# A graph network stack on one core: the RMS row sums spread by a repeated column instead of a diagonal, and the layer norm's small steps moved from VectorE to GpSimd

## The reference, cut to what matters

```python
def _layernorm(x, axis=-1, eps=1e-5):
    m = jnp.mean(x, axis=axis, keepdims=True)
    v = jnp.var(x, axis=axis, keepdims=True)
    return (x - m) / jnp.sqrt(v + eps)

# layer 0: graph convolution with degree scaling, then batch norm over all graphs
# layer 1: 8-head attention with the adjacency as its mask
# layer 2:
neighbor_sum = jnp.einsum('bnm,bmd->bnd', adjacency, x)
agg = epsilon * x + neighbor_sum
h = jnp.einsum('bnd,dh->bnh', agg, W1) + b1          # 1024 hidden features
h = jax.nn.silu(_rmsnorm(h, rms_weight))             # h * rsqrt(mean(h*h) + 1e-6) * rms_weight
out = jnp.einsum('bnh,hd->bnd', h, W2) + b2
# layer 3: 4-head graph attention
```

## Time and profile before

| | |
|---|---|
| median of 3 runs | 3986.97 us |
| lowest, highest | 3984.61, 3997.61 us |
| the profiled execution: its own time, its span | 3983.2 us, 3981.4 us |
| mean granted TensorE clock | 0.945 of full speed |
| TensorE, VectorE, ScalarE, GpSimd busy | 91%, 80%, 51%, 37% of the span |
| the chain that ended last, by engine | TensorE 76%, VectorE 13%, ScalarE 4%, DMA 2%, GpSimd 1% |

### The profile page before, as it was taken

The page is one execution under the profiler, slowest core; times in us unless marked ns, Lnnn a source line. Parts: engine busy times, 40 slices in busy tenths (PEclk is TensorE's granted clock), DMA queues, the critical chain, the costliest instruction groups (busy, mean ns, idle before and its releaser), DMA issues.

```text
span 3981.4 us, 59075 instructions
## 1 busy us (share of the span) xinstructions
PE 3629.7 (91%) x19042; PEld 2673.9 (67%) x19042; DVE 3180.7 (80%) x5637; ACT 2016.3 (51%) x3047; POOL 1473.9 (37%) x981
## 2 busy tenths in 40 slices
PE   6999478999999999999999999999999999999986
PEld 6888345666776666666676666666666766666665
DVE  6777556888888888888888888888888888888752
ACT  4665145555555555555555555555555555555430
POOL 4666233333333333333333333333333333333310
PEclk9999688999999999999999999999999999999986
DMA  8888322222222222222222222222222222222200
GB/s 286 305 309 300 93 64 64 66 67 68 56 53 59 60 69 59 63 69 69 69 69 69 69 69 69 69 69 63 69 63 52 56 57 69 62 59 69 53 16 11
DMA packets 188254, 341.08 MB, mean 86 GB/s; under 512 B 20784, under 2 KB 56496, under 8 KB 188208
## 3 DMA queue, kind: packets, MB, share of 16 engines
q1 hardware_dynamic: 188208, 340.49, 29.8%
HBM read 188.89 MB, written 50.33 MB: 60 GB/s over the span
## 4 chain that ended last, share of the span: by engine, by line
PE 76%; DVE 13%; ACT 4%; issue 3%; DMA 2%; SPq 1%; POOL 1%; DVEq 0%; ACTq 0%; POOLq 0%
PE bank L1514 12%; PE bank L1463 12%; PE obank L1396 9%; PE bank L1250 9%; PE pair L1250 7%; PE bank L1424 6%; PE pair L1380 5%; PE bank L1482 3%; PE bank L1490 3%; PE pair L1357 3%; DVE p3T L1199 3%; DVE minus_max L1047 2%; DVE diag L1113 2%; DMA pT<-in_adjT 2%; PE obank L1282 2%
## 5 line engine op out<-in xcount | busy, mean ns | idle before, releaser
L615 POOL TENSOR_TENSOR pT<-pT,node_edge 128x1024 f32<-128x1024 f32 x256 | 596.0, 2328 | 700.8 <-ACT pT L703 697.6
L1047 DVE TENSOR_REDUCE minus_max<-pair 128x2 f32<-128x1024 f32 x512 | 604.0, 1216 | 118.7 <-PE pair L1357 118.7
L1036 DVE TENSOR_TENSOR pT<-pT,node_edge 128x1024 f32<-128x1024 f32 x256 | 412.3, 1613 | 283.2 <-ACT pT L703 281.0
L703 ACT ACTIVATE pT<-pair 128x1024 f32<-128x1024 f32 x512 | 514.0, 1025 | 201.3 <-PE pair L1380 134.7
L1514 PEld LDWEIGHTS bank<-v,p3T 128*128 128x128 f32 x4096 | 509.1, 199 | 48.6 <-DVE p3T L1199 22.5
L1514 PE MATMUL bank<-v,p3T 128*128 128x65 f32 x4096 | 505.0, 280 | 19.0 <-DVE p3T L1199 18.9
L552 POOL TENSOR_TENSOR d_rs<-d_ve,minus_half 128x4 f32<-128x4 f32 x32 | 32.2, 1008 | 1263.4 <-DVE d_ve L866 1263.4
L1396 PE MATMUL obank<-pT,v 128*64 128x512 f32 x2048 | 478.0, 609 | 3.7 <-POOL pT L615 1.6
L1463 PE MATMUL bank<-w_s,hid 128*128 128x256 f32 x2048 | 479.9, 388 | 0.5 <-DVE hid L1129 0.5
L1463 PEld LDWEIGHTS bank<-w_s,hid 128*128 128x128 f32 x2048 | 382.9, 192 | 78.2 <-issue 22.1
L645 ACT ACTIVATE p3T<-x,d_sh,d_rs 128x256 f32<-128x256 f32 x128 | 66.3, 588 | 696.3 <-POOL d_sh L558 696.3
(11 more groups left out here) (190 smaller groups left out, 6413.8 us busy)
## 6 DMA issues: line engine op xcount, KB each, us to landing
pT<-in_adjT SPq DMA_DIRECT2D x64, 512.0 KB, 5.5
a_at<-in_adjT SPq DMA_DIRECT2D x64, 512.0 KB, 3.4
k_parts<-high_parts SPq DMA_DIRECT2D x256, 128.0 KB, 2.4
q_parts<-high_parts SPq DMA_DIRECT2D x256, 128.0 KB, 3.2
b_at<-in_adjT SPq DMA_DIRECT2D x64, 512.0 KB, 4.3
hid<-in_x SPq DMA_DIRECT2D x32, 512.0 KB, 4.6
x_res<-hid SPq DMA_DIRECT2D x32, 512.0 KB, 5.3
pre_bn<-hsq SPq DMA_DIRECT2D x32, 512.0 KB, 4.3
```

The lines of the kernel that those rows point to most:

```text
L615: nc.gpsimd.tensor_tensor(half, half, node_edge[:, 0:2, :], ALU.mult).then_inc(a_masked[0].sem, 1)
L703: nc.scalar.activation(dst, pair[p][:, :, :], func, **more).then_inc(a_copied[p].sem, 1)
L1036: nc.vector.tensor_tensor(half, half, node_edge[:, 2:4, :], ALU.mult).then_inc(a_masked[1].sem, 1)
L1047: nc.vector.tensor_reduce(minus_max[:, t * H1 + 2 * two_heads:t * H1 + 2 * two_heads + 2], pair[p][:, :, :], AX.X, ALU.max, negate=True).t ...
```

## The change

`b.diag` and its semaphore go. `b.spread` waits for `rrms` itself and makes four matmuls in place of one: the weights are one column of `rrms`, read 128 times over, and what moves through is the identity, so that a block of 128 columns holds the factors of its nodes on all partitions. In the layer norm, the negated mean and the variance plus epsilon are computed on GpSimd, by tensor_tensor with constant columns, in front of `power`, after a wait for the mean and variance; the copy L859 gives way to a memset of one column of a scratch tile. Two more constants are set at the start. The rest of `ORDER` stays.

```diff
-b.spread:2 a.vmask5:1 a.exp11:1 h.values20:3 a.bias:1 h.prob2:3 b.hidc5:2 a.scores71:1 b.diag:2 p.flip:0 a.exp20:1
+b.spread:2 a.vmask5:1 a.exp11:1 h.values20:3 a.bias:1 h.prob2:3 b.hidc5:2 a.scores71:1 p.flip:0 a.exp20:1
...
-        minus_half = sb("minus_half", P, T)
+        minus_half, minus_one, ln_eps = (sb(n, P, T) for n in ("minus_half", "minus_one", "ln_eps"))
+        idle_s = sb("idle_s", P, 1)
...
             def rstd(s, g):
+                pool.wait_ge(*lns[s]["mv"].upto(g, 1))
+                mean, var, rs = ln[s]["mv"][:, :, 0], ln[s]["mv"][:, :, 1], ln[s]["rs"][:, :, 0]
+                ve = ln[s]["ve"]
+                nc.gpsimd.tensor_tensor(ve[:, :, 1], mean, minus_one[:, :], ALU.mult)
+                nc.gpsimd.tensor_tensor(ve[:, :, 0], var, ln_eps[:, :], ALU.add).then_inc(lns[s]["ve"].sem, 1)
                 pool.wait_ge(*lns[s]["ve"].upto(g, 1))
-                power(ln[s]["rs"][:, :, 0], ln[s]["ve"][:, :, 0], T).then_inc(lns[s]["rs"].sem, 1)
+                power(rs, ve[:, :, 0], T).then_inc(lns[s]["rs"].sem, 1)
                 pool.wait_ge(*lns[s]["rs"].upto(g, 1))
-                nc.gpsimd.tensor_tensor(ln[s]["sh"][:, :, 0], ln[s]["ve"][:, :, 1], ln[s]["rs"][:, :, 0],
-                                        ALU.mult).then_inc(lns[s]["sh"].sem, 1)
+                nc.gpsimd.tensor_tensor(ln[s]["sh"][:, :, 0], ve[:, :, 1], rs, ALU.mult).then_inc(lns[s]["sh"].sem, 1)
...
-                nc.vector.tensor_copy(ln[s]["ve"][:, :, 1], ln[s]["st"][:, :, 1])
+                nc.vector.memset(idle_s[:, :], 0.0)
                 for t in range(T):
                     i = nc.vector.bn_aggr(out=ln[s]["mv"][:, t, :], in_=ln[s]["st"][:, t, :])
                 i.then_inc(lns[s]["mv"].sem, 1)
-                dve.wait_ge(*lns[s]["mv"].upto(g, 1))
-                mv, ve = ln[s]["mv"], ln[s]["ve"]
-                nc.vector.tensor_scalar(ve[:, :, 1], mv[:, :, 0], -1.0, None, ALU.mult)
-                nc.vector.tensor_scalar(ve[:, :, 0], mv[:, :, 1], LN_EPS, None, ALU.add).then_inc(lns[s]["ve"].sem, 1)
...
-            def b_diags(g):
-                dve.wait_ge(*b_rrms.upto(g, 1))
-                for t in range(T):
-                    i = nc.vector.tensor_scalar(diag[:, t, :], ident[:, :], rrms[:, t:t + 1], None, ALU.mult)
-                i.then_inc(b_diag.sem, 1)
...
             def b_rb(g):
-                pe.wait_ge(*b_diag.upto(g, 1))
+                pe.wait_ge(*b_rrms.upto(g, 1))
                 dst, full = b_free(g, V_RB)
-                nc.tensor.matmul(dst[:, :], ones[:, :], diag[:, :, :].rearrange("p t n -> p (t n)"),
-                                 start=True, stop=True).then_inc(full, 1)
+                for t in range(T):
+                    i = nc.tensor.matmul(dst[:, t * P:(t + 1) * P], rrms[:, t:t + 1].broadcast_to([P, P]), ident[:, :],
+                                         start=True, stop=True)
+                i.then_inc(full, 1)
```

More of the change, by code:

```diff
@@ L232, in gnn_stack @@
         w_raw = signal("w_raw", 3 + K, 16)
-        consts = signal("consts", 8)
+        consts = signal("consts", 10)
         late = signal("late", 8)
@@ L301, in gnn_stack @@
         b_rrms = signal("b_rrms")
-        b_diag = signal("b_diag")
         b_norm = signal("b_norm", KH)
@@ L525, in _ @@
             nc.gpsimd.memset(minus_half[:, :], -0.5).then_inc(consts.sem, 1)
+            nc.gpsimd.memset(minus_one[:, :], -1.0).then_inc(consts.sem, 1)
+            nc.gpsimd.memset(ln_eps[:, :], LN_EPS).then_inc(consts.sem, 1)
             nc.gpsimd.memset(e_shift[:, 0:1], E_SHIFT).then_inc(consts.sem, 1)
@@ L529, in _ @@
             nc.gpsimd.memset(sum_sq[:, :, :], 0.0).then_inc(consts.sem, 1)
-            pool.wait_ge(consts.sem, 7)
+            pool.wait_ge(consts.sem, 9)
             nc.gpsimd.affine_select(out=ident[:, :], in_=ident[:, :], compare_op=ALU.not_equal, fill=1.0, base=0,
                                     pattern=[[-1, P]], channel_multiplier=1).then_inc(consts.sem, 1)
-            pool.wait_ge(consts.sem, 8)
+            pool.wait_ge(consts.sem, 10)
             def late_consts(g, par):
@@ L841, in _ @@
         def _(dve):
-            dve.wait_ge(consts.sem, 8)
+            dve.wait_ge(consts.sem, 10)
             nc.vector.tensor_copy(bank[0][:, 0:P], ident[:, :]).then_inc(c_ident.sem, 1)
@@ L1224, in _ @@
                 **{f"a.vmask{h}": a_mask(h) for h in heads1}, **{f"a.div{k}": a_div(k) for k in range(K)},
-                "b.stats": b_ln, "b.edges": b_edges, "b.eye": b_eyes, "b.ms": b_ms, "b.diag": b_diags,
+                "b.stats": b_ln, "b.edges": b_edges, "b.eye": b_eyes, "b.ms": b_ms,
                 "b.stats3": d_ln, "b.factors": b_factors, "b.vcol": b_vcol, "b.low": b_query_low,
@@ L1235, in _ @@
         def _(pe):
-            pe.wait_ge(consts.sem, 8)
+            pe.wait_ge(consts.sem, 10)
             def flip(dst, src, k):
```

## The result

The changed kernel takes 3936.3 us (median of 4 runs, 3934.4 to 3937.2), beside 3989.6 us of the kernel before on the same chip: a ratio of **0.986**, 95% interval 0.985 to 0.988, some 53 us. The profiled execution has a span of 3932.6 us against 3981.4, 48.8 less. The forecast was 3940, with a range of 3920 to 3970.

What follows compares the result with a forecast made beforehand. TensorE, busy 91% of the span, was taken as the bound. Diagonals -45, layer 3 norm -6, first pass +3.2, filling and draining +1 made -47: 3936 from 3983.2, 3940 against the runs' median; range 3920 to 3970.

Steps and rivals of the forecast that it cites:

- The diagonals' wait: TensorE's wait before b.spread for VectorE's diagonals goes, 1.42 us a graph, 45 us together, and the gain lasts.
- Rival A: GpSimd's second mask gets in ahead of L1061, so the stall moves on: no diagonals gain, 3983 to 3987 us; chance 0.09.
- The four matmuls: b.spread's eight passes replace two: 0.2 us a graph less by the nearer row, 36 us more from above; taken as 0.
- Rival B: In b.spread the six further weight loads stand bare at 0.19 us each, giving 3976 us; chance 0.06.
- The layer norm on VectorE: L865 and L866 leave VectorE's queue: layer 3's chain to the maximum releasing L1357 shortens by 0.2 us, 6 us won.
- GpSimd's delay X: Layer norm's power starts 0.21 us later through GpSimd's two small steps; bounds near 0 and 1.25 us.
- The first pass's 3 us: Later power in the first pass's chain, some 15 passages at 0.21 us: 3.2 us lost.
- The edge of 0.42: In layer 3 of the second pass, a power delay beyond 0.42 us turns the norm's gain before L1241 into a loss.
- rival C: GpSimd's small layer norm steps cost the contended price, power 1.25 us later: 3993 us, or 4044 with another low-clock stretch; chance 0.05.
- The clock: Low stretch behind the pause before L1241: 3.4 us at 1.2 GHz, 1.7 us lost a graph; no term in the sum.
- D: The clock stays up because the pause gets 0.2 us shorter; another 51 us go, 3889 us; chance 0.06.

Runs made afterwards that it cites:

- the run pair with the clock held up: The kernel before and the changed kernel, each with eight idle matmuls added in TensorE's pause: ratios 0.985 and 0.967 to the kernel before.
- the kernels of the table: The kernel before, the changed kernel, its column and norm halves, diagonals in vain, and versions with idle matmuls; ratios from 0.967 to 1.004.
- the norm's kernel: The changed kernel with diagonals, their semaphore and the spread's single matmul put back, so only the layer norm's move remains: 3992.8 us, ratio 1.004.

## Why the prediction was right, and where its steps were off

**The diagonals' wait.** The 45 us came as reckoned, and they lasted: no wait before the values matmuls, L1061 ahead of the second mask, ScalarE's copies early. The run with the diagonals written in vain shows that this hung on VectorE's 2.7 us, as the step said. Rival A asked whether the second mask gets in first; it didn't. L1061's 0.4 us behind the first mask is what the Trainium skill, "SBUF — State Buffer", section "Who interferes with whom", leads one to expect; that it then was served before a mask ready later is what kept the gain.

**The four matmuls.** Taken as 0, though the nearer row said 0.2 us less. With the wait gone the spread takes 0.24 us a graph less (1.13 to 0.89), 7 us, but only 0.07 of it are the passes (0.96 to 0.89); the rest is that TensorE no longer starts the spread from a standstill. Rival B, bare weight loads, has nothing for it: a weight column read 128 times over costs what other weights cost (a load of L1448 takes 190 ns by the median, one of L1453 took 189).

**The layer norm on VectorE.** The step said 0.2 us shorter, and it is 0.41. I had counted the queue time of two instructions. Between the end of the last `bn_aggr` and the start of L1074 it is 0.31 less, which holds the wait for the mean and variance as well, and the memset in the place of the copy gives 0.07. Mis-sized by half, 6 us.

**GpSimd's delay X.** 0.17 for 0.21 in layer 3. The first pass's 3 us aren't shown; that more delay costs is (29 us for 0.65 us more). The edge of 0.42 doesn't follow from the step's own figures, by which the transposes wait from X = 0.26 on (2036.69 - 2036.43) and it is a loss from 0.46 on. In layer 1 the sign of rival C came up, the first of the two steps at 1.18 us by the median, but not its cost: what TensorE waits for the tile behind it (`a_xr`) in the second pass is 10.4 us, 10.3 before, once at the start. The row of the step:

```profile
L560 POOL TENSOR_TENSOR a_ve<-a_mv,minus_one x32: 200/1181/1201, 445.3 to 3600.4; 128x4 f32<-128x4 f32 x32
```

**The clock.** Here the step failed. I had the low stretch in the rows, priced it, and let it move only in rivals C and D: longer with a longer pause, gone with a shorter one. It got longer with a shorter pause. I had also read its price from one of the seven periods with the shortest stretch, 3.4 us; the mean over the 29 was 6.1 before and 8.0 after. And within the kernel before the pause is 2.5 to 2.6 us in every one of these periods, while the stretch behind it lasts from 3.4 to 10.2 us: the pause's length doesn't set the stretch's. So the sum came out right by luck in its size: a gain too small by about 7 + 6 us met a loss of about the same size that had no term. The waits and the spread alone are worth 64, the run pair with the clock held up gives 70, and the measured 47 to 53 is what the clock left.

The traces show one regularity. In the kernels of the table the stretch of 10.2 us starts between 0.3 us before and 0.1 us behind the end of the pause, that of 6.8 us from 0.2 to 2.7 us behind it, and that of 3.4 us from 2.6 to 3.8 us behind it (the second falls of the norm's kernel aside). The sooner the clock falls, the longer it stays low. What makes it fall sooner in one period than in the next, with the same work and the same pause, is open, and so is why the changed kernel has more of the early falls.

## What to carry to other kernels

A wait removed from the bounding engine is worth its length only if the engine that ended it gets its time back as well: ask what else stands behind the removed work in that queue. And a saving near a pause of TensorE should be reckoned with the clock: read the mean granted clock to three digits of both kernels, turn it into time at 1.2 GHz, and expect parts of a change not to add up until the pause is filled. Filling a pause of 2 us per 104 us with idle matmuls was worth more here (85 us) than the change itself. To compare two kernels with such a pause, compare periods that have the same time at the low clock.

## What the runs showed of the hardware that I had not expected

- Around a pause of 2.1 to 2.5 us, with two of 0.7 us behind it, TensorE went to 1.2 GHz in every one of the 29 regular periods, for a mean of 6.1 us (before) and 8.0 us (changed kernel). Eight idle matmuls, some 1.8 us of it, kept it at 2.4 GHz in 28 of 29 periods of the changed kernel and in 23 of the kernel before, but in none of the repeated column alone, where eleven did in 20. A microsecond less at 1.2 GHz gave back 0.35 to 0.36 us: 60 us for 172 us less (kernel before), 85 for some 233 (changed kernel).
- The Trainium skill, "TensorE: Matmul & The Clock Gate", section "HAM oscillation — how this bites in real kernels", describes a loop whose pause lets the clock fall in each round, with DMA waits of some 3 to 5 us as the cause. The trace agrees on the pattern, but here the pauses are waits for VectorE and only 2.1 to 2.5 us long.
- A wait of 1.4 us behind which the clock stayed up in all regular periods of the kernel before was followed by a fall in 4 of 29 with the norm's move alone. These four, at 108.8 us each, cost some 16 us, though its other periods were 0.3 us shorter than those of the kernel before. With the long pause filled, the same wait was followed by none.
